# Two-layer decoder on one core: attention outputs turned in 32x32 blocks by VectorE instead of transposed by TensorE

## The reference

```python
attn = jax.nn.softmax(scores, axis=-1)
out = jnp.einsum('bhqk,bhkd->bhqd', attn, v)
out = out.transpose(0, 2, 1, 3).reshape(B, S, D)
return out @ Wf + bf
```

## Time and profile before

| | us |
|---|---|
| median of 3 runs | 2089.47 |
| lowest and highest run | 2083.3, 2092.75 |
| span of the profiled execution, first to last instruction | 2077.8 |
| around the span, against the median of the runs | 11.7 |
| TensorE busy | 1883.8 (91%) |
| VectorE busy | 1300.3 (63%) |
| ScalarE busy | 1028.6 (50%) |
| GpSimd busy | 520.4 (25%) |

### The profile page before, as it was taken

How to read it: one execution, slowest core, us unless ns; L and a number is a source line. 1 busy time by engine, 2 the same in 40 slices (tenths; PEclk the granted TensorE clock), 3 DMA queues, 4 the chain that set the end, 5 groups by cost and what they waited for, 6 DMA issues and landing times. The chain is left out here.

```text
span 2077.8 us, 35152 instructions
## 1 busy us (share of the span) xinstructions
PE 1883.8 (91%) x12240; PEld 1099.7 (53%) x12241; DVE 1300.3 (63%) x2293; ACT 1028.6 (50%) x2008; POOL 520.4 (25%) x871
## 2 busy tenths in 40 slices
PE   8799999788689999959999999987988999995996
PEld 4344446333579999934232222253453444475995
DVE  4588874686633333367888888555587888744113
ACT  3356665577212222243677777754643666641334
POOL 3201114342233333223000000223253111143551
PEclk9899999899689999989999999998998999997998
DMA  7634403510911111055311121055035344051224
GB/s 180 143 87 67 66 3 84 118 33 9 367 49 35 34 35 33 29 162 128 68 32 32 32 46 18 1 126 107 17 79 128 49 63 63 2 203 34 71 70 145
DMA packets 99099, 158.20 MB, mean 76 GB/s; under 512 B 31447, under 2 KB 79063, under 8 KB 93783
## 3 DMA queue, kind: packets, MB, share of 16 engines
q1 hardware_dynamic: 87122, 131.79, 27.5%
q0 software_dynamic: 7488, 20.46, 3.1%
q10 hardware_dynamic: 4352, 4.20, 0.6%
HBM read 110.67 MB, written 44.72 MB: 75 GB/s over the span
## 5 line engine op out<-in xcount | busy, mean ns | idle before, releaser
L1933 ACT ACTIVATE arena<-psum 128x512 f32<-128x512 f32 (+1 forms) x1120 | 577.5, 590 | 305.6 <-PE psum L1879 210.3
L1678 DVE TENSOR_REDUCE arena<-psum 128x1 f32<-128x1024 f32 (+7 forms) x384 | 431.4, 1160 | 86.9 <-PE psum L1636 50.5
L1879 PE MATMUL psum<-arena 99*128 99x512 bf16 (+7 forms) x1280 | 369.4, 353 | 4.4 <-ACT arena L1933 2.1
L1636 PE MATMUL psum<-arena 96*128 96x512 bf16 (+7 forms) x1280 | 351.3, 358 | 23.9 <-SPq L2678 10.1
L2400 PEld LDWEIGHTS psum<-arena 128*128 128x128 f32 x2340 | 277.2, 194 | 7.4 <-ACT arena L2447 3.4
L1897 PE MATMUL psum<-arena 128*32 128x512 f32 (+3 forms) x2560 | 279.8, 537 | 0.7 <-ACT arena L1933 0.7
L2400 PE MATMUL psum<-arena 128*128 128x128 f32 x2340 | 278.3, 277 | 2.0 <-ACT arena L2447 1.4
L2493 DVE COPY arena<-arena 128x1536 f32 (+1 forms) x117 | 97.1, 831 | 285.0 <-PE psum L2400 282.5
L1664 DVE CUSTOM_DVE_ANT_0 arena<-psum,arena 128x1024 bf16<-128x1024 f32 (+3 forms) x224 | 217.6, 1021 | 53.3 <-PE psum L1636 53.0
L1879 PEld LDWEIGHTS psum<-arena 99*128 99x128 bf16 (+1 forms) x1280 | 120.5, 99 | 212.3 <-ACT arena L1933 120.7
L1636 PEld LDWEIGHTS psum<-arena 96*128 96x128 bf16 (+1 forms) x1280 | 109.3, 100 | 192.7 <-DVE arena L1678 44.3
(11 more groups left out here) (214 smaller groups left out, 2330.2 us busy)
## 6 DMA issues: line engine op xcount, KB each, us to landing
arena<-k_parts SPq DMA_DIRECT2D x144, 128.0 KB
q_halves<-arena SPq DMA_DIRECT2D x80, 192.0 KB, 2.9
arena<-q_halves SPq DMA_DIRECT2D x40, 384.0 KB, 4.9
arena<-in_L_ffn_up SPq DMA_DIRECT2D x8, 1408.0 KB, 17.6
arena<-q_halves SPq DMA_DIRECT2D x40, 256.0 KB, 5.3
k_parts<-arena SPq DMA_DIRECT2D x48, 192.0 KB, 3.2
arena<-in_L_ffn_down SPq DMA_DIRECT2D x9, 1024.0 KB, 13.3
arena<-y_rows SPq DMA_DIRECT2D x32, 256.0 KB, 4.3
```

The lines of the kernel that those rows point to most:

```text
L1636: last = nc.tensor.matmul(dst[:, base + lo:base + hi], q[0:rows, qh, h, qb % 4 * P:qb % 4 * P + P], k[0:rows, h, key0 + lo:key0 + hi], sta ...
L1678: nc.vector.tensor_reduce(dst, src, AX.X, ALU.max).then_inc(t("taken"), 1)
L1879: last = nc.tensor.matmul(b[:, at0:at0 + width], kk[0:rows, h, kb * P:kb * P + P], q[0:rows, qh, h, c0:c1], start=True, stop=diag is None)
L1933: nc.scalar.activation(probs[k % at.ahead][:, heads[0]:heads[-1] + 1, c0:c1], bank[st_bank[no % 3]][:, 0:len(heads) * width].rearrange("p ...
```

## The change

The layout of the attention output changes, and with it who turns it.
- "OC" is now on VectorE in all five attention stages: it transposes bank 7 in 32x32 blocks into `o_blk` (queries then lie on partitions within each block) and takes the reciprocal of the sums there (`Outputs.dve_take`).
- GpSimd multiplies (`pool_mix`) into `o_mix`. The two query-direction slots of a head group, 16 values wide each, sit side by side and fill the 32 columns of a block.
- "OT" is a second transpose in 32x32 blocks by VectorE, of 128x512, for every job of an odd group, 8 per stage (`dve_turn`). It writes `att_all`, the whole stage's output with features on partitions, in an order that `slots_inside` applies to the rows of the output weights on the host.
- The token stages read `att_all` straight into the projection; the row gathering, the transposes and the copies there are gone, and the projection has four banks instead of two.
- GpSimd's program in the attention stages follows `events`: splits at MT, `pool_mix` at OC, values and bias additions behind it. The bias additions of self-attention are spread over jobs 4 to 14.
- The planners count the new steps; the load of the second half of the queries (`ahead2`) no longer waits for the transposes.

The core of the diff:

```diff
+        def turn_until(time):
+            while turns and turns[0][0] <= max(free["DVE"], time):
+                mixed, j = turns.pop(0)
+                self.events.append(("OT", j))
+                free["DVE"] = max(free["DVE"], mixed) + 0.7
...
                 if end:
+                    turn_until(free["PE"] + 0.2)
                     self.events.append(("OC", j))
                     copied.append(on_dve(free["PE"] + 0.2, 0.7))
-                    outs.append(j)
-            else:
-                j = outs.pop(0)
-                free["PE"] = when + 0.45
-                self.turn["OT", j] = len(self.turn)
-                self.events.append(("OT", j))
-                taken.append(on_dve(free["PE"] + 0.2, 0.85))
+                    on_dve(0.0, 0.25)
+                    if self.jobs[j][0] % 2:
+                        turns.append((free["DVE"] + 1.0, j))
+        turn_until(float("inf"))
         self.est = max(free.values())
...
                 if packed:
+                    clip_until(free["PE"] + 0.2)
                     self.events.append(("OC", j))
-                    free["ACT"] = max(free["ACT"], free["PE"] + 0.2) + 0.65
-                    copied.append(free["ACT"])
-                    outs.append(j)
-            else:
-                j = outs.pop(0)
-                free["PE"] = when + 0.45
-                clip_until(free["PE"] + 0.2)
-                self.turn["OT", j] = len(self.turn)
-                self.events.append(("OT", j))
-                taken.append(on_dve(free["PE"] + 0.2, 0.85))
+                    copied.append(on_dve(free["PE"] + 0.2, 0.7))
+                    on_dve(0.0, 0.25)
+                    if self.jobs[j][0] % 2:
+                        turns.append((free["DVE"] + 1.0, j))
+        turn_until(float("inf"))
         self.est = max(free.values())
 
...
-        o_tok = take(NT * D)
+        o_flat = take(NT * D)
+        att_all = o_flat.rearrange("p (c t) -> p c t", c=DC)
         ats_base = top[0]
         ats = take(TPB * D).rearrange("p (t d) -> p t d", t=TPB)
-        att = take(TPB * D).rearrange("p (t c q) -> p t c q", t=TPB, c=DC)
+        late = take(TPB * D)
         w2_low = arena[:, tok_base:top[0]]
...
-        parts = take(2 * 768).bitcast(BF16).rearrange("p (s k t) -> p s k t", s=2, k=3)
+        parts_flat = take(2 * 768)
+        parts = parts_flat.bitcast(BF16).rearrange("p (s k t) -> p s k t", s=2, k=3)
+        o_mix = parts_flat[:, 0:2 * 512].rearrange("p (c b w) -> p c b w", c=2, w=32)
...
                     if source == "proj":
-                        task("ACT", "rows", p, 0.6, 0.15, ("tra", p - 4))
-                        task("PE", "tra", p, 0.55, 0.2, ("rows", p), ("att", p - 2))
-                        task("ACT", "att", p, 0.6, 0.15, ("tra", p), ("prj", p - 4))
-                        task("PE", "prj", p, 1.75, 0.2, ("att", p), ("add", p - 2))
+                        task("PE", "prj", p, 1.75, 0.2, ("add", p - 4))
...
                     if crossed:
-                        task("SP", "ahead2", 0, 1.6, 3.0, ("ahead", 0), ("tra", n_pairs - 1),
-                             *[("store", v) for v in needed[1]])
-                    free = ("att", n_pairs - 1), ("add", n_pairs - 1), *context_ends(layer)
+                        task("SP", "ahead2", 0, 1.6, 3.0, ("ahead", 0), *[("store", v) for v in needed[1]])
+                    free = ("prj", n_pairs - 1), ("add", n_pairs - 1), *context_ends(layer)
...
                     elif kind == "ahead2":
-                        sp.wait_ge(t("tra_ps"), n_pairs)
                         half_stored(sp, 1)
...
-            def pe_tra(pe, p):
-                pe.wait_ge(t("ats"), p + 1)
-                wait(pe, t("att"), p - 1)
+            def pe_prj(pe, p):
+                wait(pe, t("r"), p - 3)
                 for u in (2 * p, 2 * p + 1):
                     for c in range(DC):
-                        at0 = (u % 2) * D + c * P
-                        last = nc.tensor.transpose(bank[p % 2][:, at0:at0 + P], ats[:, u % TPB, c * P:c * P + P], ident)
-                last.then_inc(t("tra_ps"), 1)
-
-            def pe_prj(pe, p):
-                pe.wait_ge(t("att"), p + 1)
-                wait(pe, t("r"), p - 1)
-                for u in (2 * p, 2 * p + 1):
-                    for c in range(DC):
-                        last = nc.tensor.matmul(bank[2 + p % 2][:, (u % 2) * D:(u % 2) * D + D], att[:, u % TPB, c, :],
+                        last = nc.tensor.matmul(bank[p % 4][:, (u % 2) * D:(u % 2) * D + D], att_all[:, c, u * P:u * P + P],
                                                 wo[:, c, :], start=(c == 0), stop=(c == DC - 1))
                 last.then_inc(t("prj_ps"), 1)
 
...
+        class Outputs:
+
+
+            def __init__(self, at, last, rows_free=None):
+                self.at, self.last, self.rows_free = at, last, rows_free
+                self.blocks = o_blk.rearrange("p (b w) -> p b w", w=32)
+
+            def t(self, n):
+                return sem(f"att_{n}")
+
+            def dve_take(self, dve, j):
+                t = self.t
+                dve.wait_ge(t("pv"), self.last[j])
+                wait(dve, t("mixed"), j)
+                nc.vector.transpose(o_blk, bank[7][:, :]).then_inc(t("o_sb"), 1)
+                dve.wait_ge(t("o_sb"), j + 1)
+                nc.vector.reciprocal(orec2[j % 2], self.blocks[:, :, HD]).then_inc(t("rec"), 1)
+
+            def pool_mix(self, pool, j):
+                t = self.t
+                g, qh = self.at.jobs[j]
+                s, i = self.at.groups[g]
+                if j == 0 and self.rows_free:
+                    self.rows_free(pool)
+                pool.wait_ge(t("rec"), j + 1)
+                wait(pool, t("turned"), 2 * (g // 2))
+                nc.gpsimd.tensor_tensor(o_mix[:, qh, :, HD * s:HD * s + HD], self.blocks[:, :, 0:HD],
+                                        orec2[j % 2].unsqueeze(2).to_broadcast([P, 16, HD]), ALU.mult)\
+                    .then_inc(t("mixed"), 1)
+
+            def dve_turn(self, dve, j):
+                t = self.t
+                g, qh = self.at.jobs[j]
+                s, i = self.at.groups[g]
+                dve.wait_ge(t("mixed"), j + 1)
+                at0 = i % NB * S + qh * 512
+                nc.vector.transpose(att_all[:, i // NB, at0:at0 + 512],
+                                    o_mix[:, qh].rearrange("p b w -> p (b w)")).then_inc(t("turned"), 1)
+
...
-                for j in range(int(at.moved_early), 4):
-                    maxima.pool_split(pool, j)
-                for g in range(2, ng):
-                    pool.wait_ge(t("pv"), last_step[2 * (g - 2) + 1] + 1)
-                    stage_values(g)
-                    for j in (2 * g, 2 * g + 1):
-                        maxima.pool_split(pool, j)
-                if bias:
-                    add_bias(pool, *bias)
+                for e in at.events:
+                    if e[0] == "MT":
+                        maxima.pool_split(pool, e[1])
+                    elif e[0] == "OC":
+                        j = e[1]
+                        outputs.pool_mix(pool, j)
+                        if j % 2 and j // 2 + 2 < ng:
+                            pool.wait_ge(t("pv"), last_step[j] + 1)
+                            stage_values(j // 2 + 2)
+                        if bias and 4 <= j < 15:
+                            add_bias(pool, *bias, range((j - 4) * NT // 11, (j - 3) * NT // 11))
...
-            def dve_copy_out(dve, j):
-                dve.wait_ge(t("pv"), last_step[j] + 1)
-                nc.vector.tensor_copy(o_sb, bank[o_bank][:, :]).then_inc(t("o_sb"), 1)
-
-            def dve_move_out(dve, j):
-                g, qh = at.jobs[j]
-                s, i = at.groups[g]
-                turn = at.turn["OT", j]
-                dve.wait_ge(t("a_ps"), turn + 1)
-                sums = region(turn)[:, 0:512].rearrange("p (n w) -> p n w", w=32)
-                nc.vector.reciprocal(orec, sums[:, :, HD]).then_inc(t("rec"), 1)
-                dve.wait_ge(t("rec"), j + 1)
-                if j == 0 and rows_free:
-                    rows_free(dve)
-                at0 = i * (TPB * 64) + s * (2 * NB * TPB * 64) + qh * 256
-                nc.vector.tensor_tensor(o_tok[:, at0:at0 + 256].rearrange("p (n w) -> p n w", w=HD), sums[:, :, 0:HD],
-                                        orec.unsqueeze(2).to_broadcast([P, 16, HD]), ALU.mult)\
-                    .then_inc(t("taken"), 1)
-
...
-                for j in range(1, len(at.jobs)):
-                    maxima.pool_split(pool, j)
-                    if bias:
-                        add_bias(pool, *bias, (j - 1,) if j < NT - 1 else (j - 1, j))
+                for e in at.events:
+                    if e[0] == "MT":
+                        maxima.pool_split(pool, e[1])
+                    elif e[0] == "OC":
+                        j = e[1]
+                        outputs.pool_mix(pool, j)
+                        if bias and j < NT - 1:
```

(7 more changed lines are left out.)

108 lines of the change are left out of this document (33 added, 75 removed).

## The result

The changed kernel took 2075.09 us (median of 9 runs, 2068.35 to 2081.56), the kernel before 2083.3 on the same chip (9 runs, 2079.86 to 2092.75). The ratio is 0.9959, interval 0.9941 to 0.9977: 8 us faster, or 0.4%, where 2050 was forecast. That is 25 us above the forecast and still inside the stated range (2022 to 2086); by the prediction's own bound of 0.5% it is the outcome "same", which had a chance of 0.09.

A forecast was written before the change was run, and what follows sets the result against it. TensorE, with work in hand for 91% of the span, was taken to bound most attention stages, xa0 excepted. Savings 22 + 9.5 + 9 - 1 = 39.5 us off 2077.8 give 2038.3; with 11.7 around it 2050 us, range 2022 to 2086.

The forecast's parts named there:

- part 4: VectorE and ScalarE inside attention stages: added VectorE load is hidden, 118.6 of 136.8 us in xa0; counted as nothing.
- Part 1: Attention stages: removing TensorE's output transposes saves 22 us, about 5 each in at0, at1, mla, xa1 and 2 in xa0.
- Parts 2 and 3: Token stages: removed transposes save 9.5 us; seams after attention stages: shorter serial chain saves 1.8 us each, 9 in all.
- Part 5: GpSimd's queue, tight in xa0: a product ahead of a split of maxima holds it 0.63 us; 1 us charged.
- "Another order": Rival, planners' random search: orders differ everywhere, draws as good are likely, worse ones could eat the gain; 2085 us, chance 0.06.
- "Other engines take over the pace": Rival: TensorE arrives earlier and waits for exp, reductions and norms; only 20 us off, 2069, chance 0.14.
- The "slower" rival: Rival, GpSimd's queue: splits wait behind products, 1.6 us each, 59 us for half the jobs; 2109, chance 0.11.
- the clock rival: Rival: emptier stretches lower TensorE's granted clock, 12 us lost; 2062, chance 0.05.
- The 11.7 us "around the span": Whole kernel: the profiled span, 2077.8 us, lay 11.7 below the runs' median; added back to the forecast.

The follow-up runs named there:

- b1: Kernel before, with TensorE transposing each attention output twice (8 transposes instead of 4); 2101.37 us, ratio 1.0088.
- u2: y4 with the planners' seed 3 instead of 1; 2035.78 us, ratio 0.9788.
- y1: Kernel before, with the cross-attention planner pricing the landing of the maxima at 7.0 instead of 5.0 us; 2064.25 us, ratio 0.993.
- z1: y1 with the output bank copied by VectorE instead of ScalarE in cross-attention; 2078.49 us, ratio 0.9994.
- u3: y4 with the second turn in xa0 taking only 32 of its 512 columns, same orders; 2043.5 us, ratio 0.9837.
- y4: Changed kernel with cross-attention bias additions behind the split, maxima landing priced 7.0 us, and an early GpSimd drain in at1; 2049.24 us, ratio 0.9848.
- v1: u2 with the landing of the maxima priced 9.0 instead of 7.0 us; 2032.98 us, ratio 0.9781.
- x1: Changed kernel, with GpSimd's cross-attention bias additions behind the next split instead of behind the product; 2073.18 us, ratio 0.9947.
- u1: y4 with the planners' seed 2 instead of 1; 2040.39 us, ratio 0.9818.

## Why the prediction was wrong

The forecast took 39.5 us off, and the pair on record shows 8.2. Over three draws of the planners it is 17, and with the landing of the maxima priced 7.0 on both sides 20, beside the covered drain. By stage, change in us (from the profiled executions; the stages that the change does not touch are left out, and scatter by some us):

| | forecast | pair on record | mean of three draws | the same, landing 7.0, bias, drain |
|---|---|---|---|---|
| at0 | -5 | -8.7 | -8.8 | -7.5 |
| xa0 | -2 | +7.3 | +4.8 | +11.5 |
| at1 | -5 | +3.8 | +0.6 | -6.2 |
| xa1 | -5 | +6.4 | +1.7 | -5.5 |
| mla | -5 | 0 | -3.1 | -3.8 |
| t1, t2, t4, t5, t6, with the seams | -18.5 | -16.2 | -15.9 | -14.7 |
| GpSimd's queue | +1 | | | |
| sum | -39.5 | -7.4 | -20.7 | -26.2 |

The last column has what was forecast everywhere but in xa0. **The step that failed is part 4, the load of VectorE in xa0, which it put at nothing**; beside it, the drain at the end of at1 (5.7 us), which no part had, and an order with too short a price, which hit the changed kernel harder in xa1.

*Part 1, transposes in the attention stages (22 us).* The sum held: b1 gives 18 to 21 us for 80 groups. Its shares did not: in b1 a group weighs more in at0 and at1 (7.8 and 9.6 us for 16) and nothing in xa0. In at0 the gain is 8.6 us for the 5.0 of the step, and it is there with every seed (245.3 and 243.9 against 253.3 and 253.5). In at1 the distance between the first scores of neighbouring jobs fell from 23.8 to 23.45 us in the steady part, 15 x 0.35 = 5.2, as the step had it. But the first job was 2.2 us longer (29.4 for 27.2 us, and 29.2 to 29.5 with the other seeds), and the drain took 5.7 more. In mla a pair of jobs fell from 30.0 to 29.4 us; in the pair on record longer jobs here and there took that back, and u2 has it. The 5 us of xa1 are there once the order is right (5.5). The 2 us of xa0 never were.

*Parts 2 and 3, token stages and seams (18.5).* Nearly right. The seam's 1.9 us falls into the token stages (inside at0 the end after the last PV is 2.5 us for 2.2), so t1, t2, t4, t5 and t6 answer for all of it: 16.3 us shorter, and 16 over the means of three seeds. t6 gained nothing in the pair, and 2.5 over the three seeds.

*Part 4, VectorE (nothing).* The load was right (119.2 us in xa0, forecast 118.6), and it was not hidden. The step said "118.6 in xa0 of 136.8", with room left in the sum. The 28 us of room were not room: y1 took 14 us out of the stage without touching VectorE's work, and what was left could take none of it. z1 put 8.9 us on VectorE there and the stage became 9.0 longer. This is shown for the kernel before with VectorE's copy, in one draw against three within 0.9 us; for the changed kernel u3 leaves it open. "The next job's first PV waits for the turn as it waited for the copy" names a place where little is lost: in y4's xa0 TensorE's waits for the turn sum to 4.0 us, in y1's those for the copy to 4.9. The planners do count VectorE's steps, and run with the price of 7.0 their own estimate of xa0 is 132.3 us for the kernel before, 140.5 for z1 and 137.2 for the changed kernel: the cost that the step put at nothing stood in the build. What makes the changed kernel's xa0 (133.9 to 136.0) 2 to 4 us longer than z1's is open. The transfer is not it (v1). Late splits may be: with the price of 7.0, 5 of the 15 splits of y4's xa0 start 0.55 to 1.67 us after their negation, behind a product or a bias addition.

*Part 5, GpSimd (1 us).* The mechanism was named, for xa0, and the size was off, for xa1: 1.12 us in 6 of 15 splits, 3 to 5 us (x1). That the bias addition stands behind the product, and doubles the hold, was in the code before and not counted. The Trainium skill (GPSIMD Engine Reference, Key points) has VectorE about twice as fast at elementwise work; by an estimate from it the product would take twice VectorE's 0.426, 0.85. The rows have 0.651, so the trace does not agree at this size. The stretching to 1.2 us that I feared doesn't show in its mean.

*What no part had.* The 6.5 us by which GpSimd's drain outlasts its work at the end of at1. The row of before that could have warned is GpSimd's idle gap of 19.38 us across the end of at1: the change moved work of GpSimd to the very end of a stage, and I priced the work and not the barrier behind it.

*The rivals.* "Another order" had a chance of 0.06 because "draws as good are likely, for the costs hardly change". With the seeds 2 and 3 the gain would have been 20 to 22 us instead of 8. The reason given is true of the kernel before (2083.3, 2080.6, 2081.5) and not of the changed one. Why that is so was only argued: in its orders bank, clips and maxima all pass through one engine, and small shifts may count more. "Other engines take over the pace" (2069) describes xa0. The "slower" rival's mechanism, splits behind products, is real, at a tenth of the price it gave. The clock fell as the clock rival said, from 0.91 to 0.86 in xa0. It went along with TensorE's waits: with the price of 7.0 it is 0.97 in the kernel before (y1) and 0.91 to 0.94 in the changed one (y4, u1, u2).

*The baseline.* The forecast was made against 2089.47; the same kernel's median was 2083.3 beside the changed one, and 2078 to 2081 later. So the miss is 25 us in the time and 31 in the gain. The 11.7 us "around the span" were misread as the start and end of the program: where an execution's time and span are both known they differ by some 2 us (2075.09 and 2073.4 for the changed kernel). The rest is that the profiled execution was faster than the median. That the forecast's 2050 agrees with y4's 2049 is luck.
